# One value product per step, low keys copied by GpSimd, a scalar operand and a shorter router chain

## The reference

```python
xn   = layernorm(x)                                # x: 16 x 512 x 128
q,k,v = xn @ Wq/Wk/Wv + b                          # 16 heads of 64
att  = softmax(causal(q @ k.T / 8)) / 8
attn = concat_heads(att @ v) @ proj
base = xn @ W.T
lw   = softmax(l2norm(xn @ Wp.T + bp) @ l2norm(sim) * scale)   # 4 experts
ret  = lw where the first argmax, else 0
res  = sum_e ret[e] * (xn @ Wd[e].T @ Wu[e].T)     # ranks 1, 2, 4, 8
out  = x + attn + base + res
```

## Time and profile before

| | us |
|---|---|
| three runs | 1508.14, 1509.38, 1512.44 |
| median | 1509.38 |
| the profiled execution, by the same clock | 1512.81 |
| its span in the trace | 1511.0 |
| TensorE busy | 1431.5 (95%) |
| VectorE busy | 1188.9 (79%) |
| ScalarE busy | 1058.7 (70%) |
| GpSimd busy | 810.5 (54%) |
| mean granted TensorE clock | 0.983 |

### The profile page before, as it was taken

One profiled execution on the slowest core, in us unless ns is written; L12 is line 12 of the kernel. 1 busy time (PEld: TensorE's weight loads), 2 busy tenths in 40 slices (PEclk: granted clock), 3 DMA queues, 4 the chain that ended last, 5 costly groups with the idle time before them and its releaser, 6 DMA issues.

```text
span 1511.0 us, 40243 instructions
## 1 busy us (share of the span) xinstructions
PE 1431.5 (95%) x11036; PEld 1167.3 (77%) x11036; DVE 1188.9 (79%) x4294; ACT 1058.7 (70%) x3032; POOL 810.5 (54%) x1137
## 2 busy tenths in 40 slices
PE   5999999999999999999999999999999999999998
PEld 4778778777787777878778787777877778777886
DVE  5787868879688796887868779787797878879785
ACT  4677767767677776776767767676776767767775
POOL 4555545555455554555545555564555645555553
PEclk8999999999999999999999999999999999999999
DMA  6545555545445545554545545545554554555552
GB/s 159 118 113 134 119 127 125 121 117 132 120 113 126 133 115 123 127 130 108 125 119 125 126 109 127 129 114 134 117 127 112 131 126 113 126 124 126 126 126 57
DMA packets 133424, 184.33 MB, mean 122 GB/s; under 512 B 22271, under 2 KB 51262, under 8 KB 133310
## 3 DMA queue, kind: packets, MB, share of 16 engines
q1 hardware_dynamic: 133310, 183.25, 51.0%
HBM read 11.20 MB, written 4.19 MB: 10 GB/s over the span
## 4 chain that ended last, share of the span: by engine, by line
PE 80%; DVE 6%; SPq 6%; DMA 4%; issue 3%; ACT 1%; DVEq 0%; ACTq 0%
PE zp L1061 20%; PE ptp L1037 15%; PE jobp L951 12%; PE scores L1025 11%; PE scores L1028 9%; PE outp L1073 6%; PE jobp L956 5%; DMA k_low<-k_lo 3%; SPq L410 3%; DVE prob L777 2%; SPq L416 1%; PE jobp L966 1%; DVE lg L863 1%; DVE k_lo L674 1%; SPq L419 1%
## 5 line engine op out<-in xcount | busy, mean ns | idle before, releaser
L511 POOL TENSOR_TENSOR prob<-prob,rden 128x128 f32<-128x128 f32 (+3 forms) x1024 | 713.1, 722 | 671.7 <-DVE rden L766 671.7
L777 DVE CUSTOM_DVE_ANT_0 prob<-scores,mask 128x128 f32<-128x128 f32 (+3 forms) x1024 | 461.7, 484 | 294.0 <-issue 248.2
L581 ACT ACTIVATE prob<-prob,nmax 128x128 f32<-128x128 f32 (+3 forms) x1024 | 565.1, 555 | 128.6 <-DVE nmax L777 125.4
L1037 PE MATMUL ptp<-ident,prob 128*128 128x128 f32 x2560 | 385.0, 277 | 6.8 <-DVE pt L789 6.4
L1025 PE MATMUL scores<-k_twice,q_parts 128*128 128x128 f32 (+3 forms) x1024 | 334.9, 337 | 48.1 <-DMA k_low<-k_lo 35.6
L1037 PEld LDWEIGHTS ptp<-ident,prob 128*128 128x128 f32 x2560 | 297.8, 141 | 50.1 <-POOL prob L511 27.0
L592 ACT ACTIVATE pt<-ptp 128x128 f32<-128x128 f32 (+3 forms) x512 | 222.0, 434 | 146.8 <-PE ptp L1037 131.8
L1028 PE MATMUL scores<-k_low,q_parts 128*128 128x128 f32 (+3 forms) x1024 | 323.1, 325 | 0.0
L1061 PE MATMUL zp<-pt,v_sb 128*64 128x64 f32 (+3 forms) x4096 | 322.3, 313 | 0.0
L1025 PEld LDWEIGHTS scores<-k_twice,q_parts 128*128 128x128 f32 x1024 | 193.9, 189 | 117.7 <-issue 43.2
L1061 PEld LDWEIGHTS zp<-pt,v_sb 128*64 128x64 f32 x4096 | 231.6, 143 | 55.1 <-issue 26.4
(11 more groups left out here) (140 smaller groups left out, 1663.4 us busy)
## 6 DMA issues: line engine op xcount, KB each, us to landing
k_twice<-k_hi SPq DMA_DIRECT2D x512, 128.0 KB, 2.4
q_parts<-q_hi SPq DMA_DIRECT2D x256, 128.0 KB, 2.4
q_parts<-q_lo SPq DMA_DIRECT2D x256, 128.0 KB, 2.4
k_low<-k_lo SPq DMA_DIRECT2D x256, 128.0 KB, 2.4
xin<-in_L_attn_x_dram SPq DMA_DIRECT2D x16, 256.0 KB, 3.3
xres<-in_L_attn_x_dram SPq DMA_DIRECT2D x16, 256.0 KB, 2.9
out_dram<-osb SPq DMA_DIRECT2D x16, 256.0 KB, 2.5
pt<-in_L_attn_Wq_dram SPq DMA_DIRECT2D x1, 512.0 KB, 4.3
```

Source lines behind the costliest of these rows:

```text
L511: nc.gpsimd.tensor_tensor(part, part, scale, ALU.mult).then_inc(pn_ready, 1)
L581: nc.scalar.activation(part, part, ACT.Exp, bias=nmax[:, s % NROT, h:h + 1], scale=-1.0, accum_out=den[:, s % NROT, h:h + 1]).then_inc(p_r ...
L777: nc.vector.tensor_tensor_reduce(out=prob[:, s % NROT, h, 0:cols], in0=scores[h][:, 0:cols], in1=mask[:, S - cols:S], scale=-INV_SCALE, sc ...
L1037: done = nc.tensor.transpose(ptp[h][:, P * j:P * j + P], prob[:, s % NROT, h, P * j:P * j + P], ident[:])
```

## The change

The two heads' value products are no longer issued in one step: head 0's at s % 4 = 0, head 1's at s % 4 = 1. The joint copy out of `zp` by ScalarE and VectorE comes one step later, s % 4 = 2. The value jobs of steps 1, 5, 9, 13, 17 go to steps 2, 6, 10, 14, 18 (the other PSUM bank) and the router from 6 to 5. The two DMAs of the low keys go from SyncE's queue; GpSimd copies the halves instead, after it has normalised that step's unit, each on 64 partitions and 512 elements, and TensorE waits for that as well. GpSimd's scaling takes the reciprocal as a per-partition scalar operand of `tensor_scalar`. In the router each expert gets eight columns (zero padded), so that gating is one operation and not four; ties are broken by a descending ramp, a maximum and a comparison in place of seven small operations; the clamp and root of the norm go to GpSimd as one power of -1/2; the chain ends four half steps earlier. The diff, cut (a line of "..." is left out text; functions stand in the order SyncE, GpSimd, ScalarE, VectorE, TensorE):

```diff
-RSUM = sum(RANKS)
+RMAX = max(RANKS)
-NRD = PROJ + RSUM
-RPAD = 48
-PARTS, PART = 3, 32
+PARTS, PART = 3, NEXP * RMAX
+NRD = PROJ + PART
...
-LAG_PV = 8
-LAG_Z = 9
+LAG_PV = (8, 9)
+LAG_Z = 10
...
-JOBS[6] = ("router", 0)
+JOBS[5] = ("router", 0)
-V_STEPS = (29, 30, 1, 5, 9, 13, 17, 21)
+V_STEPS = (29, 30, 2, 6, 10, 14, 18, 21)
-COPIES = {"q": 4, "k": 6}
+KEY_AHEAD = max(_s for _s in JOBS if JOBS[_s][0] == "k")
+COPIES = {"q": 4, "k": 4}
-R_CHAIN = 20
+R_CHAIN = 14
...
-                sp.wait_ge(job_done[bank], c.job(s))
-                for h in range(2):
-                    if kind == "q":
+                if kind == "q":
+                    sp.wait_ge(job_done[bank], c.job(s))
+                    for h in range(2):
                         sp.dma_start(q_parts[other(h), h, n % 2, :].bitcast(F32),
                                      q_lo[own(h), n % 2, :].bitcast(F32)).then_inc(moved, 16)
-                    else:
-                        sp.dma_start(k_low[own(h), h, n % 2, :].bitcast(F32),
-                                     k_lo[own(h), :].bitcast(F32)).then_inc(moved, 16)
...
+            nc.gpsimd.memset(small_in[:, 1:3, :], 0.0).then_inc(zeroed, 1)
+            for e in range(NEXP):
+                nc.gpsimd.memset(ramp[:, :, e:e + 1], float(NEXP - e)).then_inc(zeroed, 1)
...
+            def pad_low_keys(c, s, setup=False):
+                n = JOBS[s][1]
+                made = c.fixed(c.job(s))
+                scaled = 0 if setup else c.fixed(c.head(s, 1))
+                pool.wait_ge(zeroed, 8 + NEXP)
+                if not setup:
+                    pool.wait_ge(pn_ready, scaled)
+                pool.wait_ge(job_done[bank_of(s)], made)
+                for h in range(2):
+                    nc.gpsimd.tensor_copy(k_low[own(h), h, n % 2, :], k_lo[own(h), :].bitcast(F32))\
+                        .then_inc(low_padded, 1)
+                pool.wait_ge(low_padded, c.values(n + (NPAIR if s in AHEAD else 0), 1))
+
+            pad_low_keys(Counts(pool, -1), KEY_AHEAD, setup=True)
...
-                    scale = rden[:, s % NROT, h:h + 1].to_broadcast([P, width(s)])
-                    nc.gpsimd.tensor_tensor(part, part, scale, ALU.mult).then_inc(pn_ready, 1)
+                    nc.gpsimd.tensor_scalar(part, part, rden[:, s % NROT, h:h + 1], None, ALU.mult)\
+                        .then_inc(pn_ready, 1)
...
-                        nc.gpsimd.tensor_tensor(unorm[:, 1, :], unorm[:, 0, :], power[:, 1, :], ALU.pow)\
+                        nc.gpsimd.tensor_scalar(unorm[:, 1, :], unorm[:, 0, :], L2_EPS_SQ, None, ALU.max)\
+                            .then_inc(unorm_clamped, 1)
+                        pool.wait_ge(unorm_clamped, c.at(1, 1))
+                        nc.gpsimd.tensor_tensor(unorm[:, 2, :], unorm[:, 1, :], power[:, 0, :], ALU.pow)\
                             .then_inc(unorm_root, 1)
...
                     normalise(c, s)
+                    if s in JOBS and JOBS[s][0] == "k" and not (last and s in AHEAD):
+                        pad_low_keys(c, s)
...
-                act.wait_ge(pv_ready, c.pair(p))
+                act.wait_ge(pv_ready, c.values(p, 1))
-                    wait(act, pv_ready, c.pair(p - 2))
+                    wait(act, pv_ready, c.values(p - 2, 0))
-                    wait(dve, pv_ready, c.pair(p - 2))
+                    wait(dve, pv_ready, c.values(p - 2, 1))
...
+                if t == 18:
+                    prior(8)
+                    nc.vector.tensor_tensor(ranked, chosen, ramp[:], ALU.mult).then_inc(r_chain, 1)
+                if t == 19:
+                    prior(9)
+                    nc.vector.tensor_reduce(row[:, 4, :], ranked, AX_X, ALU.max).then_inc(r_chain, 1)
+                if t == 20:
+                    prior(10)
+                    nc.vector.tensor_tensor(first, ranked, over_experts(row[:, 4, :]), ALU.is_ge)\
+                        .then_inc(r_chain, 1)
+                if t == 21:
+                    prior(11)
+                    nc.vector.tensor_tensor(routed, weights, first, ALU.mult).then_inc(r_chain, 1)
+                if t == 22:
+                    prior(12)
+                    nc.vector.tensor_tensor(gated[:].rearrange("p n (e r) -> p n e r", r=RMAX),
+                                            dn[:].rearrange("p n (e r) -> p n e r", r=RMAX),
+                                            routed.unsqueeze(3).to_broadcast([P, NBLK, NEXP, RMAX]), ALU.mult)\
+                        .then_inc(r_chain, 1)
+                if t == 23:
+                    prior(13)
+                    nc.vector.tensor_copy(gated_parts[:, :, 0:PARTS:2, :],
+                                          gated[:].unsqueeze(2).to_broadcast([P, NBLK, 2, PART])).then_inc(r_chain, 1)
+                if t == 24:
+                    prior(14)
+                    nc.vector.tensor_tensor(gated_parts[:, :, 1, :], gated[:],
+                                            gated_parts[:, :, 0, :].bitcast(F32), ALU.subtract)\
                         .then_inc(gated_ready, 1)
...
+                    pe.wait_ge(low_padded, c.values(p, 1))
...
-                p = due(s, LAG_PV, NBLK, first, tail)
-                if p is not None:
-                    values(c, p)
+                for h in range(2):
+                    p = due(s, LAG_PV[h], NBLK, first, tail)
+                    if p is not None:
+                        values(c, p, h)
```

More of the change, by code:

```diff
@@ L505, in normalise @@
             def normalise(c, s):
[L507 removed]
+                summed = c.fixed(c.unit(s))
+                pool.wait_ge(consts_ready, 3)
+                pool.wait_ge(r_ready, summed)
                 for h in range(2):
                     part = prob[:, s % NROT, h, 0:width(s)]
[L510 to L511 removed]
+                    nc.gpsimd.tensor_scalar(part, part, rden[:, s % NROT, h:h + 1], None, ALU.mult)\
+                        .then_inc(pn_ready, 1)
             def batch(b, last):
@@ L813, in router @@
                 t -= R_FIRST
-                logits, shifted, exps, weights, chosen, routed = (lg[:, n, :, :] for n in (1, 2, 3, 4, 5, 6))
-                taken = row[:, 4, :]
+                logits, shifted, exps, weights, chosen, ranked, first, routed = (lg[:, n, :, :] for n in range(1, 9))
                 if t == 0:
@@ L867, in router @@
-                if t == 25:
-                    prior(17)
-                    nc.vector.tensor_tensor(routed, weights, chosen, ALU.mult).then_inc(r_chain, 1)
-                if t == 26:
-                    prior(18)
-                    r0 = 0
-                    for e, r in enumerate(RANKS):
-                        last = nc.vector.tensor_tensor(gated[:, :, r0:r0 + r], dn[:, :, r0:r0 + r],
-                                                       lg[:, 6, :, e:e + 1].to_broadcast([P, NBLK, r]), ALU.mult)
-                        r0 += r
-                    last.then_inc(r_chain, 1)
@@ L1039, in transpose, with values @@
                     done.then_inc(t_ready, 1)
-            def values(c, p):
-                wait(pe, z_ready, c.pair(p - 1))
-                if p in (0, NPAIR // 2):
+            def values(c, p, h):
+                pe.wait_ge(pt_ready[h], c.unit(NBLK * p + NBLK - 1))
+                if h == 0:
+                    wait(pe, z_ready, c.pair(p - 1))
+                if h == 0 and p in (0, NPAIR // 2):
                     for bank in range(2):
```

98 lines of the change are left out of this document (40 added, 58 removed).

## The result

| | before | after |
|---|---|---|
| median, us | 1509.33 (1508.14 to 1512.44, 4 runs) | 1485.51 (1484.91 to 1487.89, 4 runs) |
| the profiled execution | 1512.81 | 1484.91 |
| its span | 1511.0 | 1482.8 |
| mean granted clock | 0.983 | 0.998 |

What follows compares the result with a forecast made beforehand. TensorE, busy 95%, was taken as the bound. Boundaries -23, clock -18, second value block +34, delays -54 and start -4 us gave -65, so about 1445 us as a median; range 1415 to 1482.

Steps and rivals of the forecast that it cites:

- Scaling with a scalar operand ... worth 0: GpSimd's 512-wide scaling takes 0.5 to 1.04 us; off the chain, so any saving is worth 0.
- low keys: At loop boundaries, fewer SyncE copies cut the stall from 2.07 to 0.7 us; first four steps 11.5 us, 23 us less.
- clock: In the four steps behind a boundary's first four, the granted clock no longer falls; 18 us less.
- start: At the kernel's start and in the first batches, one low-key wait and two short ones go; 4 us less.
- the router: In the pair that ends the router, 1.5 of 2.0 us of delay go per batch; 24 us less.
- the split: Separating the value products adds 34 us for second blocks and returns 30 us of delays outside the router's share: +4.
- rival of a full GpSimd: If a scalar operand costs twice the product's 1.04 us, GpSimd becomes the bound; above 1560 us, chance 0.03.
- GpSimd's two copies: Low-key copies on GpSimd take 0.5 us each, 1.1 us a pair, and cost nothing.
- Second value block: In each pair, TensorE pays 0.30 us at the ends of a second block of value products; 34 us more.
- Delays returned: Per batch, 0.65 us in two ordinary pairs, 0.4, 0.2 and the router's 1.5 in others; 54 us less.
- GpSimd's scalings holding up the transposes: A sign that would show the forecast wrong: TensorE's transposes delayed by GpSimd's scalings; no size given.
- The port rule of the Trainium skill: Two-input VectorE instructions wait for GpSimd's SBUF reads; would cost 20 of the router's 24 us; set aside.

Runs made afterwards that it cites:

- e6_dma: The kernel after the change, scalar operand kept, with the low keys back on SyncE's DMA queue and GpSimd's copies gone; 1486.05 us.
- e1_tt: The kernel after the change, with GpSimd's scaling put back to the two-input product with a broadcast operand; 1441.56 us.
- e7: The kernel before the change, with only GpSimd's copies of the low keys added; 1476.71 us.
- e3: e1_tt with both heads' value products in one step again; 1457.05 us.
- e2_before_scalar: The kernel before the change, with only GpSimd's scaling switched to the scalar operand; 1503.28 us.
- e8_before_router: The kernel before the change, with only the shorter router chain; 1475.21 us.
- e5_tt_dma: e1_tt with the low keys back on SyncE's DMA queue and GpSimd's copies gone; 1468.20 us.
- e9_late_root: The kernel after the change, with VectorE's three router links behind the root moved four half steps later; 1486.67 us.

## Why the prediction was wrong, point by point

- **The step that failed is "Scaling with a scalar operand ... worth 0".** Its bounds of 0.5 to 1.04 us were both below what it costs, 1.56, because the nearest row was taken for the one-input cast of 1024 elements and that is another loop; and GpSimd off the chain was read as a time worth 0 in either direction. It said "and beyond if the operand is expensive", yet gave that no price in the sum or the range. It costs 43.9 us here (1485.51 - 1441.56). Without it the measured time is 1441.6, where 1445 was forecast; that this comes so close is in part luck, as three errors cancel: low keys, clock and start were to give 45 us and gave 32.6, the router 24 and gave 19.7 behind them, and the split was to cost 4 (leaving the router's share of the delays out) and gave 15.5.
- **The rival of a full GpSimd** named the right engine and asked the wrong question, when it is full. It was to decide at twice the product's time, 2.1 us, and give over 1560. The loss set in at 1.5 times, with a mean load of 91% (81% in e6_dma, 17.9 us): GpSimd never became the bound, but its queue is late at the places at which others meet it. Its chance of 0.03 was too small by far, and "nothing but the missing row speaks for it" was reason enough for more. That unit 1's scaling sits behind the copies was named; that the router's root sits behind six scalings was not.
- **Low keys.** The stall shrank from 2.07 to 0.25 us in the row shown, forecast 0.7; P0 is 10.80 us (10.50 in e1_tt) where 11.5 was taken and an ordinary pair was the bound. The copies alone bring 1.45 us (e7 11.71), with a stall of 0.81 us as a median; that is near the two issues (2 x 0.6 + 0.1 = 1.3, so the lower bound of 0.8 for them does not follow from the earlier trace rows). VectorE's earlier return from the branch, which moved SyncE's queue 1 us forward, comes on top and belongs to the router's part (10.68 in e3).
- **Clock.** Right: 0.998, and no fall in P1. One shorter stall is enough, and either of two parts shortens it: as a median it is 1.81 us in e2_before_scalar, where the clock fell behind twelve boundaries, and 1.22 in e8_before_router, where it fell behind one.
- **GpSimd's two copies.** 0.61 us each, forecast 0.5. Costing nothing was right in e1_tt, where P4 and P5 are as long as in e5_tt_dma. It was wrong in e7 with joint value products (0.61 us a batch in P4 and P5), and with the scalar form (0.5 us left of 26.6).
- **Second value block.** 0.25 to 0.44 us a pair for 0.30. Row for row: the weight loads idle 0.17 and 0.38 us about each block, as in the earlier trace rows.

```profile
745.70 0.86 PEld L1084 LDWEIGHTS zp<-pt,v_sb 128*64 128x64 f32 x16 [0.17 <-issue]
746.94 0.19 PEld L973 LDWEIGHTS jobp<-xt_hi,w_hi 128*128 128x128 f32 x1 [0.38 <-issue]
...
748.97 0.86 PEld L1084 LDWEIGHTS zp<-pt,v_sb 128*64 128x64 f32 x16 [0.17 <-issue]
750.21 0.19 PEld L1048 LDWEIGHTS scores<-k_twice,q_parts 128*128 128x128 f32 x1 [0.38 <-issue]
```

- **Delays returned.** P3 and P4 were right in e1_tt (10.39 for 10.4); P4, P5 and P6 returned more than forecast. The sign that was named as wrong, "GpSimd's scalings holding up the transposes", is hardly there in the change (1.6 us): its P3 of 11.55 hangs on the root. It shows in e9_late_root (11.7 us) and in e2_before_scalar (16.9 us).
- **Router.** 34.3 us alone and 19.7 behind the copies, for 24; the place was wrong: the forecast put 1.5 us in P6, where it is 0.3. The port rule of the Trainium skill was set aside because the comparisons average 0.37 us "beside scalings of that length". That reading was wrong. None of the 48 started under a scaling: 33 started beside no GpSimd instruction and took 0.16 us, 15 under the layer norm's product and took 0.84, ending 0.02 us behind it. The gating products, which did start under scalings, average 529 ns, and the shortest takes 154. The rule did not cost 20 of the 24 us either. It struck in the wide cast of P6: 848 ns with the short chain alone, against 282 for the one cast that started before the product.

The sum, re-made from the runs: copies -32.6 (before to e7), router -19.7 (e7 to e3), split -15.5 (e3 to e1), scalar operand +44.0 (e1 to after) = -23.8.

## What to carry to other kernels

An operation whose form no row shows has no upper bound from a row of another form: on the engine that is to take on more work besides, price it from above, and ask where that engine is late for something that others wait for, not when it is full; its mean load does not tell (81% cost 17.9 us in one kernel, 85% cost 9.1 in another). A wait for a side product (here a root of 128x4) behind a busy in-order queue delays everything queued behind the waiting instruction; moving the reader shifted that, and here only less work in the queue mended it. A mean over a group hides its two kinds of instruction: look at which of them ran beside what. Try the parts of a bundled change one at a time: here one of four took away more than any other gave.

## What the hardware showed that was not expected

On GpSimd a product with a per-partition scalar takes 1.5 times as long as the same product with a broadcast tensor operand (1563 and 1045 ns for 128x512), and still 1.4 times with a constant (1489).

VectorE's short operations wait out some of GpSimd's instructions and not others. In the kernel before, every one of the 64 gating products started under a two-input scaling of GpSimd, and they took from 0.15 to 1.02 us; the median one ended 0.07 us behind that scaling. With the scalar form alone exchanged, page row of e2_before_scalar and its VectorE:

```profile
PE 1428.3 (95%) x11036; PEld 1166.2 (78%) x11036; DVE 1150.9 (77%) x4294; ACT 1059.1 (71%) x3032; POOL 1195.7 (80%) x1137
...
L865 DVE TENSOR_TENSOR lg<-lg,row 128x4 f32<-128x4 f32 x48 | 7.6, 159 | 0.0
```

VectorE's comparisons take 159 ns, not 371, since none of them meets the layer norm's product any more. The 16 that started under a scalar-form scaling took 159 to 162 ns and ended 0.4 to 0.5 us before it. So did, in 154 to 158 ns, the 15 that started under the layer norm's power of 128x4, a two-input operation of GpSimd that takes 1 us. So these comparisons and the gating products waited out GpSimd's wide two-input products, and hardly its scalar form (the gating products average 169 ns beside it), though that reads SBUF as well. The section of the Trainium skill named above says that a VectorE instruction with two SBUF inputs contends with a GpSimd instruction that reads SBUF; the layer norm's product bears that out, the scalar form does not, and the measurement decides. VectorE saved 1188.9 - 1150.9 = 38 us, which is the likely reason why e2_before_scalar is 4.6 us faster in spite of the transposes that wait for it (argued, not tested alone).
